# Ten instructions fewer a sequence in TensorE's list, and 70 signals ahead of the layers

## What is computed

```python
h = layernorm(x) * (1 + ca) + sa
x = x + ga * causal_attention(h)                 # 16 heads of 8, rotary embedding
h = layernorm(x) * (1 + cb) + sb
x = x + gb * local_transformer(h)

def local_transformer(x):
    for i in range(6):                           # DEPTH
        t = shift_tokens(x)
        q, k, v = split(t @ Wqkv[i])             # 128 -> 3 x 1024, 16 heads of 64
        q, k = l2norm(q) * qs[i], l2norm(k) * ks[i]
        q, k = rotary(q), rotary(k)              # with a scale by place
        # each window of 32 tokens looks at itself and the window before
        a = softmax(where(mask, -big, 8 * q @ k.T)) @ v
        x = a @ Wo[i] + x
        xn = layernorm(shift_tokens(x)) * g[i] + b[i]
        a, gate = split(xn @ W1[i] + b1[i])      # 341 each
        x = (a * gelu(gate)) @ W2[i] + b2[i] + x
    return x
```

## Time and profile before

| | |
|---|---|
| median of three runs | 3702.66 us |
| profiled execution, first to last instruction (span) | 3699.1 us |
| PE busy | 3521.4 us, 95% |
| DVE busy | 3039.5 us, 82% |
| ACT busy | 2586.6 us, 70% |
| POOL busy | 2309.1 us, 62% |
| granted TensorE clock, mean | 0.987 |

### The profile page before, as it was taken

How to read it: one execution, slowest core, us unless ns; L and a number is a source line. 1 busy time by engine, 2 the same in 40 slices (tenths; PEclk the granted TensorE clock), 3 DMA queues, 4 the chain that set the end, 5 groups by cost and what they waited for, 6 DMA issues and landing times. The chain is left out here.

```text
span 3699.1 us, 146879 instructions
## 1 busy us (share of the span) xinstructions
PE 3521.4 (95%) x63940; PEld 2694.0 (73%) x63940; DVE 3039.5 (82%) x4947; ACT 2586.6 (70%) x4028; POOL 2309.1 (62%) x1364
## 2 busy tenths in 40 slices
PE   6999996999999999999999999999999999999996
PEld 4777774777777777777777777777777777777774
DVE  5767766988889988888888888888898888888883
ACT  3565554677777777777777777777777777777773
POOL 1110104767777777777777767777777777776761
PEclk9999998999999999999999999999999999999998
DMA  2000001212222222222222222222222222222212
GB/s 75 4 4 7 4 7 43 56 48 58 56 58 63 64 56 58 56 56 62 58 56 58 54 56 64 56 58 55 64 63 58 56 57 54 56 56 54 54 49 68
DMA packets 121989, 188.76 MB, mean 51 GB/s; under 512 B 24942, under 2 KB 43142, under 8 KB 120972
## 3 DMA queue, kind: packets, MB, share of 16 engines
q1 hardware_dynamic: 121356, 179.36, 18.7%
HBM read 24.08 MB, written 4.19 MB: 8 GB/s over the span
## 5 line engine op out<-in xcount | busy, mean ns | idle before, releaser
L1325 POOL TENSOR_TENSOR rc<-rc,rs 128x1024 f32<-128x1024 f32 x384 | 912.9, 2377 | 349.2 <-DVE rs L1391 348.5
L1331 POOL TENSOR_TENSOR rc<-rc,rnorm 128x1024 f32<-128x1024 f32 x384 | 723.7, 1906 | 392.9 <-DVE rnorm L162 331.4
L1385 DVE TENSOR_TENSOR rc<-proj,rope_b 128x1024 f32<-128x1024 f32 x384 | 466.7, 1215 | 96.1 <-ACT squares L1177 89.6
L1177 ACT ACTIVATE squares<-proj 128x1024 f32<-128x1024 f32 x384 | 394.0, 1026 | 151.1 <-PE proj L921 137.6
L1013 PEld LDWEIGHTS ring<-pT,vmoved 64*64 64x64 f32 x18432 | 381.2, 135 | 132.8 <-issue 132.8
L1391 DVE TENSOR_TENSOR rs<-proj,rope_b 128x1024 f32<-128x1024 f32 x384 | 466.2, 1214 | 0.0
L958 PEld LDWEIGHTS ring<-ident,rc 128*128 128x128 f32 x3072 | 364.2, 142 | 137.5 <-issue 52.2
L1399 DVE TENSOR_REDUCE sums<-squares 128x16 f32<-128x1024 f32 x384 | 455.3, 1186 | 1.1 <-issue 0.9
L1013 PE MATMUL ring<-pT,vmoved 64*64 64x32 f32 x18432 | 407.7, 220 | 37.9 <-issue 36.4
L958 PE MATMUL ring<-ident,rc 128*128 128x128 f32 x3072 | 426.3, 277 | 11.6 <-POOL rc L1331 6.6
L1013 PE MATMUL ring<-pT,vown 64*64 64x32 f32 x6144 | 381.9, 219 | 13.8 <-issue 13.8
(11 more groups left out here) (176 smaller groups left out, 7886.1 us busy)
## 6 DMA issues: line engine op xcount, KB each, us to landing
vmoved<-vown SPq DMA_DIRECT2D x576, 128.0 KB
vmoved<-vown SPq DMA_DIRECT2D x192, 192.0 KB
vmoved<-vown SPq DMA_DIRECT2D x576, 64.0 KB
wqkv_raw<-in_L_ffn_Wqkv SPq DMA_DIRECT2D x40, 192.0 KB, 2.7
wo<-in_L_ffn_Wo SPq DMA_DIRECT2D x6, 512.0 KB, 4.2
x_attended<-xtok SPq DMA_DIRECT2D x8, 256.0 KB, 2.0
xtok_c<-x_attended SPq DMA_DIRECT2D x8, 256.0 KB, 4.2
out<-xtok_c SPq DMA_DIRECT2D x8, 256.0 KB, 2.4
```

The costliest lines, as they stand in the source:

```text
L1177: nc.scalar.activation(squares[:, c, :], proj[c][:, :], ACT.Square).then_inc(sq_done, 1)
L1325: nc.gpsimd.tensor_tensor(rc[:, k % 2, c, :], rc[:, k % 2, c, :], rs[:, c, :], ALU.add).then_inc(add_done, 1)
L1331: nc.gpsimd.tensor_tensor(dst, dst, rnorm[:, k % 2, c * HEADS:(c + 1) * HEADS].rearrange("p (h o) -> p h o", o=1).broadcast_to([P, HEADS, ...
L1385: nc.vector.tensor_tensor(rc[:, k % 2, c, :].rearrange("p (h d) -> p h d", h=HEADS), proj[c][:, :].rearrange("p (h d) -> p h d", h=HEADS), ...
```

## The change

The change has four parts, all on PE in `part_b`:

- 70 signals (`pe_passed`) at the head of the block's PE list, ahead of its first wait.
- `proj_emptied` no longer waits for `sq_done`; `project` has that wait by itself.
- `weigh` signals `pe_passed` once a tile and not twice.
- two waits for `gated`, in `feed_down` and ahead of `output`, stand only where there is no next tile.

```diff
+FETCH_SHIFT = 70
...
         @block.tensor
         def _(pe):
+            for _ in range(FETCH_SHIFT):
+                pe.sem_inc(pe_passed, 1)
             pe.wait_ge(zeroed, 6)
...
             def proj_emptied(c, k):
 
-                u = 2 * min(k, NT - 1) + c + 1
-                pe.wait_ge(turned_done, u)
-                pe.wait_ge(sq_done, u)
+                pe.wait_ge(turned_done, 2 * min(k, NT - 1) + c + 1)
...
                 if k:
                     proj_emptied(c, k - 1)
+                    pe.wait_ge(sq_done, 2 * (k - 1) + c + 1)
...
                     pe.wait_ge(moved, (k + 1) * 7 * 16)
+                    pe.sem_inc(pe_passed, 1)
                 banks = [ring_bank(f"O{i}", k)[:, :].rearrange("p (q k) -> p q k", q=PAIRS) for i in range(2)]
-                pe.sem_inc(pe_passed, 1)
...
                 pe.wait_ge(w2_in, 32 * (n // BATCH + 1))
-                pe.wait_ge(gated, 3 * n + 3)
+                if not tile(g + 1):
+                    pe.wait_ge(gated, 3 * n + 3)
...
                 if seq_at(g, 5) is not None:
-                    if rest is not None:
+                    if rest is not None and not tile(g + 1):
                         pe.wait_ge(gated, 3 * rest + 1)
                     output(seq_at(g, 5), 1, g)
```

## The result

The kernel after takes **3608.23 us** (median of four runs, 3606.61 to 3608.65), the kernel before, run on the same chip, 3703.28 us (four runs, 3693.33 to 3711.20). The ratio is 0.9737, with a 95% interval of 0.9715 to 0.9758: 95 us less. The forecast was 3612, within 3600 to 3635. The four runs of after lie within 2.0 us, those of before within 17.9.

What follows compares the result with a forecast made beforehand. PE bounds the kernel, stopping where 256-instruction blocks of its list come late. Terms 90.2 - 1 + 2 = 91 us off the 3699.1 span give 3608, with 3.6 around it 3612 us; range 3600 to 3635.

Steps and rivals of the forecast that it cites:

- What bounds the kernel: PE sets the pace, and stops where a 256-instruction block of its list comes late; 61.8 us in 82 pieces.
- Part 1: Sequences 2 to 46: ten instructions fewer each lock the phase in the quick band, 60.9 us each; 90.2 us less.
- Part 2: Sequences 0 and 1, before the lists are regular: +1 us, between -3 and +4.
- Part 3: Last sequence and drain: stops before L1013 and L979 go, -2 us.
- Part 4: The ten removed waits and signals a sequence themselves: taken as 0, at most 24.5 us gained at 51 ns each.
- Part 5: The 70 signals ahead of the layers: 3.6 us, hidden in 10.7 free us, so 0; uncovered 3.6 to 7.
- Around the span: Time outside the profiled span: 3.6 us, the median of runs 3702.7 against the span 3699.1, added to the forecast.
- A: Rival: edges don't matter or something else shares their period; stops stay, most likely 3700 us; chance 0.04.
- B: Rival: phase locked where edges are bad in every sequence; +36 us, 3739 us, worst single one +106; chance 0.05.
- C: Rival: a stop makes the next block late, so sequences are quick only after quick ones; 3657 us; chance 0.06.
- That the time varies less: Run times after should vary less than before's 3693 to 3704 us, block lateness being partly chance.

Runs made afterwards that it cites:

- e5: Changed kernel with 326 signals in front instead of 70, the same phase one block later; 3647.56 us.
- e1: Changed kernel with no signals in front instead of 70, phase locked at 86; 3771.35 us.
- e2: Changed kernel with 161 signals in front instead of 70, phase 247; 3770.82 us.
- e12: Changed kernel with 110 signals in front instead of 70, phase 196; 3680.23 us.
- e6: Changed kernel with 45 signals in front instead of 70, phase 131; 3608.23 us.
- e10: Changed kernel with 203 signals in front instead of 70, phase 33; 3667.30 us.
- e4: Kernel before, sq_done and gated waits kept, cut to 2,560 instructions a sequence by fewer signals and one score matmul, 76 signals in front; 3607.02 us.
- e9: e4 with 53 signals in front instead of 76, phase 131 in weigh; 3608.43 us.
- e3: Changed kernel with no signals in front and ten signals a sequence in place of the removed instructions, 2,570 again, sliding phase; 3681.32 us.
- e11: e4 with 211 signals in front instead of 76; 3701.30 us.
- e8: e1 with every vmoved transfer cut to one of eight head pairs, the rest zero; 3769.35 us.

## Why the prediction was right

**What bounds the kernel** was read rightly: PE, and the stops at edges of its list. That the edges have a period of 256 is shown by e5; that they and not something else of the same period are at work, by e1, e2 and e12, where nothing but the number of signals ahead of the layers differs from after, and the time moves by up to 163 us. The traces say the same by the place of the stops. Counted with two places for each weight load and its matmul and one for each wait or signal, 79 of 81 stops of before from 740 us on stand on one remainder modulo 256 or its neighbours, and so do 93 of 95 in e1, 121 of 123 in e2 and 81 of 83 in e12, on the same remainder in all four. The signals in front moved the work against the edges, and the stops stayed with the edges.

**Part 1**, the 45 sequences: -90.2 forecast, -88.0 measured. 60.95 us each instead of 60.91, and the layer's end as priced (306.1 for five with one in them). Its choice of 60.9, the quick sequence of before, carried the whole prediction. It had a side effect that the part didn't name and yet held: taking a whole quick sequence instead of taking off the 61.8 us of stops brought in the 27 us of busy time. Taking off the stops alone would have given 26 us too little. What the runs show of the 27 us: the clock's halvings after stops are among them (six of 3.4 us, in each of which PE does half the work, so about 6 x 1.7 = 10 us as an estimate from these rows). Most of the rest is how a stop is shown. One of before:

```profile
1563.51 0.22 PE L1013 MATMUL ring<-pT,vown 64*64 64x32 f32 x1
1564.35 0.26 PE L1013 MATMUL ring<-pT,vmoved 64*64 64x32 f32 x5 [0.62 <-issue]
```

The matmul ahead of the stop counts as busy for its whole 0.22 us, while in the run the next one begins some 0.02 us behind it. PE's work stands still for 0.84 us, and 0.62 of it is called idle. 82 stops of 0.2 us are some 16 us, an estimate from these rows; with the 10 of the clock that is nearly all of the 27.

**Part 2**, sequences 0 and 1: +1 forecast, -3.8 measured, just beyond its bound of -3. The phases were counted rightly (57 and 188), but their stops came to 1.8 us instead of 4.4. A phase alone doesn't set what a sequence costs, as e6, e10 and e12 show too.

**Part 3**, the last sequence: -2 forecast, -2.8 measured.

**Part 4**, the waits themselves: nothing forecast. e4 (3607.02) and e9 (3608.43) confirm it for the kernel after. It would have been wrong for a kernel whose edges stop: there the waits are worth 18 us (e3 against before) or 33 (e10 against e11). The upper bound of 24.5 us, from 51 ns each, was the wrong quantity: in e11 the 33 us come with 48 more stops in score, not with 51 ns a wait. That the wait makes the block late is argued below, not shown.

**Part 5**, the 70 signals: the term that was furthest off in size, and it came to nothing by luck. "Even at twice 51 ns the signals are done": signals that follow one another take 0.153 us each (e2 and e5), three times 51 ns. 70 of them are 10.7 us, not 3.6, and 10.7 us was free. The signals in after, and PE's first L920:

```profile
L906 PEldq EVENT_SEMAPHORE  x70: 51/51/51, 588.8 to 599.4; - x70
```

```profile
599.66 0.77 PE L920 MATMUL proj<-wqkv_hi,xa_hi 128*128 128x512 f32 x1 [12.05 <-POOL xa_lo L1310]
```

against 599.30 in the earlier trace rows. The 69 steps from 588.8 to 599.4 us are 0.154 us each. The releaser named is still POOL, but the last signal begins at 599.4, behind the 599.30 at which before could begin: the cover was used up. The signals cost 0.3 us, and each one more would have cost its 0.15, as e2 and e5 do. Without the cover they would have cost 10.7 us and not the 3.6 to 7 given. The 51 ns of the earlier trace rows were the shown length of a record, not the pitch at which they follow one another.

**Around the span** it is 1.8 us in after's profiled run (3606.61 against a span of 3604.8), not 3.6; the 3.6 compared the span of one execution of before with the median of others. The forecast was 3.8 us too high: 3.3 by the sum (-94.3 for -91) and 1.8 by what lies around the span, less 1.6 by which the median of after is above its profiled run; rounding is the rest.

**The rivals.** A (the edges don't matter) is refuted by e1, e2 and e5. B (locked to a bad phase) didn't happen, but e1 and e2 are exactly that kernel, at 3771 us: more than the 3739 given, within the +106 of the worst sequence. Its price was taken from the mean of slow sequences of before; a locked sequence at 86 takes 62.5 to 68.7 us, while 81 and 91 in before, passed once, took 62.6 and 64.2. C (a stop once begun makes the next block late) is refuted for after: all 45 sequences are quick, although sequence 0 and 1 had stops. That the time varies less, as said, is so: 2.0 us against 17.9.

The rule of the Trainium skill that crossing a block's edge is mostly hidden (Runtime: NRT & Kernel Launch, section Instruction fetch mechanics) doesn't hold for this kernel: e1 and after, which differ in nothing but 70 signals ahead of the layers, are 163 us apart by where the edges fall. At the phases 131 and 156 the traces agree with it.

**What stays open.** First, why phases 131 to 177 are quick. The times of the packets on q8 show how near a block is, with the edges counted in the traces. At the stops of before, e1 and e2 PE goes on 1.2 to 1.7 us after the end of the block's transfer, which itself takes 0.9 to 2.0 us. In after the last transfer has ended at least 1.9 us before PE comes to an edge, at each of the 450 edges of the steady part. Two things bring a block nearer than that. One is a short block: all 77 stops of e12 from 760 to 3500 us end a block whose work takes PE 2.1 to 2.4 us, while the shortest in after takes 4.3. The other is a transfer that begins late: in after it mostly begins 0.7 to 1.0 us after PE's array passes an edge, but 2.6 to 6.1 us after it at all 50 stops of e10, whose blocks hold 4.4 us of work or more.

What delays the start isn't shown. Waits of PE's sequencer of more than 0.3 us may be part of it: from 600 us on they fill 496 us of e1, and 22 of its 480 transfers begin in one; in e2 it is 1 of 481. But in after it is 90 of 481, in 526 us of waits, so a wait doesn't keep a transfer from beginning. What before, after, e1 and e2 have in common is that none begins more than 0.9 us into a wait. In e1 147 transfers begin 1.0 to 1.3 us after the end of such a wait and 46 in the first 0.9 us. At one place of the list, the same in e1 and e8, a wait of 2.13 us ends 6.2 us after the edge, and the transfer begins 7.2 us after it. This would fit a sequencer that asks for the next block between waits, and it would explain why the ten waits cost time just where blocks are tight. It is an argument from times that go together; no kernel took it apart.

Second, before was slow at 127, where e6 and e9 locked at 131 are quick: the history of a sliding phase may count, or four places; not settled.

## What to carry to other kernels

When a loop body of small instructions shows "issue" pauses on the bounding engine, count the instructions between them. If nearly all pauses stand on one remainder of the size of a block (256 here), suspect that the list's blocks come late; then the body's length and its start matter beside its work. A phase is safe where each transfer ends well before its block is needed (1.9 us or more in after). Cutting the body to whole blocks locks the phase for better or worse: 95 us gained at one shift and 72 us lost at another, so the shift has to be measured, and a body whose phase slides lay in the middle (3681 and 3699 us between 3608 and 3771). Price a removed stall by whole good stretches of the trace, not by the idle time alone, and price fillers by the pitch at which they follow one another, not by their shown length.

## What the runs showed of the hardware that was not expected

- Signals on PE's sequencer that follow one another take 0.153 us each (e2 against e5; 0.154 by the 70 of after), though each is shown with 51 ns.
- A block's lateness doesn't depend on how many bytes the other DMAs move: with 47 MB on q1 instead of 179, in as many packets, the stops at L1015 are 100.2 us against 97.1 (e8, e1).
- In before, after, e1 and e2 no transfer of the list's blocks begins more than 0.9 us into a wait of PE's sequencer; in the first 0.9 us it is 22 of 480 in e1, 1 of 481 in e2 and 90 of 481 in after.
- A stop of 1.8 us in a dense run can be followed by some 3.4 us at half the granted clock (0.61 in the stretch shown under e1). The 21 such pieces of e1's steady part are some 36 of the 63 us of busy time that it has more than after, an estimate by half the work in each.
- Waits whose condition others imply cost nothing at a good phase (e4, e9) and 33 us at a bad one (e11 against e10).
